# Top-two expert choice of 14 of 16 batches taken out of the routing and made in the last batch's attention

## What is computed

```
h = layernorm(x) * (1 + ca) + sa
x = x + ga * attention(h)                      # softmax attention, per batch
h = layernorm(x) * (1 + cb) + sb
logits = h @ Wr + br                           # 8192 tokens x 8 experts
top_vals, top_idx = top_k(logits, 2)
w = softmax(top_vals)                          # two weights per token
key = where(expert was chosen, w, -1e30)       # 8 x 8192 in effect
kv, ki = top_k(key, 1280)                      # each expert's tokens
y = (gelu(h[tok] @ W1 + b1) @ W2 + b2) * gate  # scattered back and added
x = x + gb * layernorm(y_sum + h) ...
```

## Time and profile before

| what | value |
| --- | --- |
| time, median of 3 runs | 1362.34 us (1360.73 to 1362.84) |
| time of the profiled execution | 1361.43 us |
| its span | 1359.7 us |
| busy: TensorE, VectorE, ScalarE, GpSimd | 86%, 73%, 56%, 71% of the span |
| granted TensorE clock, mean | 0.917 of full |

### The profile page before, as it was taken

The page is one execution under the profiler, slowest core; times in us unless marked ns, Lnnn a source line. Parts: engine busy times, 40 slices in busy tenths (PEclk is TensorE's granted clock), DMA queues, the critical chain, the costliest instruction groups (busy, mean ns, idle before and its releaser), DMA issues. The chain is left out here.

```text
span 1359.7 us, 23684 instructions
## 1 busy us (share of the span) xinstructions
PE 1163.7 (86%) x5975; PEld 786.6 (58%) x5976; DVE 989.6 (73%) x2189; ACT 757.9 (56%) x1494; POOL 958.7 (71%) x1096
## 2 busy tenths in 40 slices
PE   7899999999999999999999999999972175989400
PEld 6456566665656666665656666665542175989400
DVE  4888687777768777777767777776637894767596
ACT  4665666566566766666566765666422531444244
POOL 4686978888796878878697878879651135545268
PEclk9999999999999999999999999999985556999755
DMA  4000101011010101011010101010014203233374
GB/s 152 17 19 17 57 8 63 3 62 42 20 47 16 63 0 62 16 47 47 16 47 16 62 0 48 8 42 32 17 47 132 70 0 94 46 95 47 93 251 165
DMA packets 68478, 70.91 MB, mean 52 GB/s; under 512 B 12912, under 2 KB 64032, under 8 KB 68272
## 3 DMA queue, kind: packets, MB, share of 16 engines
q1 hardware_dynamic: 46800, 47.18, 10.9%
q10 hardware_dynamic: 16896, 16.78, 3.7%
q0 software_dynamic: 4704, 6.11, 3.0%
HBM read 40.35 MB, written 29.45 MB: 51 GB/s over the span
## 5 line engine op out<-in xcount | busy, mean ns | idle before, releaser
L627 ACT ACTIVATE PF<-PS 128x512 f32<-128x512 f32 x512 | 298.2, 595 | 256.6 <-PE PS L1002 248.4
L894 DVE TENSOR_REDUCE NMAX<-PS 128x1 f32<-128x512 f32 x512 | 342.7, 682 | 87.7 <-PE PS L1011 84.4
L490 POOL TENSOR_TENSOR SF<-SF,PF 128x512 f32<-128x512 f32 x252 | 321.9, 1298 | 14.9 <-ACT PF L627 14.7
L1083 PE MATMUL PS<-PF,V 128*64 128x512 f32 x1024 | 248.0, 605 | 0.0
L1001 PE MATMUL PS<-Q,K 128*128 128x512 f32 x512 | 222.1, 434 | 2.7 <-ACT PF L627 2.6
L1011 PE MATMUL PS<-K,Q 128*128 128x512 f32 x512 | 205.6, 403 | 10.4 <-DVE NMAX L894 10.3
L1002 PE MATMUL PS<-Q,K 128*128 128x512 f32 x512 | 201.3, 393 | 0.0
L646 ACT ACTIVATE Q<-PS 64x512 fp32r<-64x512 f32 x256 | 151.5, 592 | 47.5 <-PE PS L102 42.5
L568 POOL TENSOR_TENSOR XL<-XF,XH 128x512 fp32r<-128x512 f32 x63 | 82.6, 1311 | 128.1 <-ACT XH L701 128.1
L1001 PEld LDWEIGHTS PS<-Q,K 128*128 128x128 f32 x512 | 96.3, 188 | 120.2 <-issue 55.2
L487 POOL TENSOR_TENSOR SF<-PF 128x512 f32<-128x512 f32 x126 | 162.0, 1301 | 2.9 <-ACT PF L627 2.9
(11 more groups left out here) (329 smaller groups left out, 2501.1 us busy)
## 6 DMA issues: line engine op xcount, KB each, us to landing
X<-in_L_attn_x SPq DMA_DIRECT2D x16, 512.0 KB, 3.5
MODB<-mod_rows SPq DMA_DIRECT2D x16, 512.0 KB, 3.7
h_rows<-H ACTq DMA_DIRECT2D x16, 512.0 KB, 3.0
acc_rows<-H ACTq DMA_DIRECT2D x16, 512.0 KB, 4.1
out_x<-X SPq DMA_DIRECT2D x16, 512.0 KB, 2.9
A<-acc_rows SPq DMA_DIRECT2D x15, 512.0 KB, 8.7
W1F<-in_L_ffn_W SPq DMA_DIRECT2D x3, 1024.0 KB, 5.0
W2F<-in_L_ffn_W SPq DMA_DIRECT2D x3, 1024.0 KB, 7.3
```

The costliest lines, as they stand in the source:

```text
L490: s_sum.done(pool.tensor_tensor(total, total, tile, ALU.add))
L627: s_exp.done(act.activation(PF[:, u % 8, :], st_bank(u), ACT.Exp))
L894: s_mred.done(dve.tensor_reduce(NMAX[:, p % 2, r:r + 1], mx_bank(u), AX.X, ALU.max, negate=True))
L1083: last = pe.matmul(num_bank(p)[odd * R:(odd + 1) * R, :], V1[:, vp, c, :], PF[:, k % 8, :], start=(c == 0), stop=(c == TC - 1))
```

## The change

- `LOGITS` is now laid out as 4 chunks x 16 batches x 8 experts, so that a range of batches is a slice of it; L884 writes at that stride.
- The top-two chain is a class `TopTwo` of 20 steps, 0 to 19, over a range of batches. Its last step writes the keys over the logits; `KEY` is gone.
- `early` does batches 0 to 13 (448 elements wide, 56 narrow) in the attention: steps 0 to 12 in body 15, one a slot from slot 19, and steps 13 to 19 in body 16, slots 0 to 3, two a slot. Its tiles lie in tiles of the attention that are free by then. Each step stands at the start of its slot on VectorE, ahead of the slot's jobs and divisions, and waits for the step before. Its exponential is in ScalarE's body 15, slot 28.
- `late` does batches 14 and 15 in the routing, in 64 elements wide, 8 narrow.
- The keys are released by one semaphore increment after the last step. TensorE and SyncE read them from `LOGITS`.
- GpSimd waits at the start of the routing until the last batch's H2 has been read by its transfers (`s_h2out`).

```diff
+EARLY = NB - 2
+class TopTwo:
+    STEPS, EXP_FROM, EXP_TO = 20, 7, 12
+    def exponential(self, act):
+        act.wait_ge(self.s_dd, 1)
+        act.activation(self.ex, self.den, ACT.Exp).then_inc(self.s_exp, 1)
+    def step(self, dve, k, link):
+        L, eq, oh1, oh2, l2 = self.logits, self.eq, self.oh1, self.oh2, self.l2
+        if k == 0:
+            link(dve.tensor_reduce(self.m1, L, AX.X, ALU.max))
+        elif k == 1:
+            link(dve.tensor_tensor(eq, L, self.each(self.m1), ALU.is_equal))
+        elif k == 2:
+            link(dve.tensor_tensor(eq, eq, self.rank, ALU.mult))
+        elif k == 3:
+            link(dve.tensor_reduce(self.i1, eq, AX.X, ALU.max))
+        elif k == 4:
+            link(dve.tensor_tensor(oh1, self.rank, self.each(self.i1), ALU.is_equal))
+        elif k == 5:
+            link(dve.scalar_tensor_tensor(out=l2, in0=oh1, scalar=-3.0e38, in1=L, op0=ALU.mult, op1=ALU.add))
+        elif k == 6:
+            link(dve.tensor_reduce(self.m2, l2, AX.X, ALU.max))
+        elif k == 7:
+            link(dve.tensor_tensor(self.den, self.m2, self.m1, ALU.subtract))
+            dve.sem_inc(self.s_dd, 1)
+        elif k == 8:
+            link(dve.tensor_tensor(eq, l2, self.each(self.m2), ALU.is_equal))
+        elif k == 9:
+            link(dve.tensor_tensor(eq, eq, self.rank, ALU.mult))
+        elif k == 10:
+            link(dve.tensor_reduce(self.i2, eq, AX.X, ALU.max))
+        elif k == 11:
+            link(dve.tensor_tensor(oh2, self.rank, self.each(self.i2), ALU.is_equal))
+        elif k == 12:
+            dve.wait_ge(self.s_exp, 1)
+            link(dve.tensor_scalar(self.den, self.ex, 1.0, None, ALU.add))
+        elif k == 13:
+            link(dve.reciprocal(self.w1, self.den))
+        elif k == 14:
+            link(dve.tensor_tensor(self.w2, self.ex, self.w1, ALU.mult))
+        elif k == 15:
+            link(dve.tensor_tensor(eq, oh1, oh2, ALU.add))
+        elif k == 16:
+            link(dve.tensor_tensor(oh1, oh1, self.each(self.w1), ALU.mult))
+        elif k == 17:
+            link(dve.tensor_tensor(oh2, oh2, self.each(self.w2), ALU.mult))
+        elif k == 18:
+            link(dve.tensor_tensor(oh1, oh1, oh2, ALU.add))
+        elif k == 19:
+            link(dve.scalar_tensor_tensor(out=L, in0=eq, scalar=-1.0, in1=oh1, op0=ALU.add, op1=ALU.add))
...
+    TOP_AT, TOP_EXP = [(NB - 1, 19 + k) for k in range(13)] + [(NB, k // 2) for k in range(7)], (NB - 1, 28)
...
+                    if at == TOP_EXP:
+                        early.exponential(act)
...
+                    for k in [k for k in range(TopTwo.STEPS) if TOP_AT[k] == at]:
...
+                        early.step(dve, k, top)
                     normalise(b, n, 0)
...
     @block.gpsimd
     def _(pool):
+        m["s_h2out"].wait(pool, NB - 1, 1)
         pool.memset(ONES[:, :], 1.0).then_inc(s_pool, 1)
...
-        sp.wait_ge(s_key, TC)
+        sp.wait_ge(s_key, 1)
...
-            sp.dma_start(rows[q], KEY[:, q, :, :]).then_inc(s_tab, 16)
+            sp.dma_start(rows[q], LOGITS[:, q, :, :]).then_inc(s_tab, 16)
...
+        for k in range(TopTwo.STEPS):
+            late.step(dve, k, link)
+        dve.sem_inc(s_key, 1)
         dve.wait_ge(s_pool, POOL_CONSTS)
-        for q in range(TC):
-            dve.scalar_tensor_tensor(out=KEY[:, q, :, :], in0=EQ[:, q::TC, :], scalar=-1.0, in1=OH1[:, q::TC, :],
-                                     op0=ALU.add, op1=ALU.add).then_inc(s_key, 1)
```

More of the change, by code:

```diff
@@ L83, in wait, with __init__, each @@
         eng.wait_ge(self.sem, b * 8 + (16 - 8 * self.parity))
+class TopTwo:
+    STEPS, EXP_FROM, EXP_TO = 20, 7, 12
+    def __init__(self, m, batches, wide, small, s_dd, s_exp):
+        self.b, self.n = batches, batches.stop - batches.start
+        self.logits = m["LOGITS"][:, :, batches, :]
+        self.eq, self.oh1, self.oh2, self.l2 = (x.rearrange("p (q b e) -> p q b e", q=TC, e=E) for x in wide)
+        self.m1, self.m2, self.i1, self.i2, self.ex, self.w1, self.w2, self.den = (x.rearrange("p (q b) -> p q b", q=TC) for x in small)
+        self.rank = m["RANK8"][:, :].unsqueeze(1).unsqueeze(1).broadcast_to([P, TC, self.n, E])
+        self.s_dd, self.s_exp = s_dd, s_exp
+    def each(self, x):
+        return x.unsqueeze(3).broadcast_to([P, TC, self.n, E])
+    def exponential(self, act):
[45 more added lines that the diff above has]
+            link(dve.scalar_tensor_tensor(out=L, in0=eq, scalar=-1.0, in1=oh1, op0=ALU.add, op1=ALU.add))
@@ L120, in build_program @@
         m["IDENT"] = sb("IDENT", [P, P])
[L121 removed]
+        m["LOGITS"] = sb("LOGITS", [P, TC, NB, E])
         m["SAME"], m["LOWER"] = sb("SAME", [P, P]), sb("LOWER", [P, P])
@@ L231, in attention @@
     EPSC, HALF, ONE5, NEG1 = (m[x] for x in ("EPSC", "HALF", "ONE5", "NEG1"))
+    n4, n1 = TC * EARLY * E, TC * EARLY
+    flat = [x[:, :, :].rearrange("p k n -> p (k n)") for x in (NF, XN1)]
+    s_top = sem("s_top")
+    early = TopTwo(m, slice(0, EARLY), [x[:, j * n4:(j + 1) * n4] for x in flat for j in range(2)],
+                   [LTF[:, j * n1:(j + 1) * n1] for j in range(8)], sem("s_topd"), sem("s_tope"))
+    TOP_AT, TOP_EXP = [(NB - 1, 19 + k) for k in range(13)] + [(NB, k // 2) for k in range(7)], (NB - 1, 28)
     streams = []
@@ L761, in finish @@
                         dve.tensor_tensor(H2[:, c, :], H2[:, c, :], MODB[:, 2, :], ALU.add).then_inc(s_hadd2, 1)
-            chain, mask, pad = Chain(dve, s_dset), Chain(dve, s_mask), Chain(dve, s_keypad)
+            chain, mask, pad, top = Chain(dve, s_dset), Chain(dve, s_mask), Chain(dve, s_keypad), Chain(dve, s_top)
             pad(dve.memset(K2[R:P, :, :].bitcast(F32), 0.0))
@@ L1122, in route @@
     FAR = 4.0 * NT
-    EQ, OH1, OH2, L2 = (sb(x, [P, NCH, E]) for x in ("EQ", "OH1", "OH2", "L2"))
-    KEY = sb("KEY", [P, TC, NS, E])
-    M1, M2, I1, I2, EX, W1, W2, DEN = (sb(x, [P, NCH]) for x in ("M1", "M2", "I1", "I2", "EX", "W1", "W2", "DENr"))
+    EQ, n1 = sb("EQ", [P, NCH, E]), TC * (NB - EARLY)
+    wide, small = [sb(x, [P, n1 * E])[:, :] for x in ("EQt", "OH1", "OH2", "L2")], [
+        sb(x, [P, n1])[:, :] for x in ("M1", "M2", "I1", "I2", "EX", "W1", "W2", "DENr")]
     HI, LO, LOW, SGN, EQT, RANK, SEL, SCAN, DST, ZT = (
@@ L1161, in route @@
     m["s_tab"] = s_tab
+    late = TopTwo(m, slice(EARLY, NB), wide, small, sem("s_rtopd"), s_exp)
     kt_ps = PS[:, 0, :]
@@ L1205, in _ @@
         act.activation(iot_ps, IOT[:, :], ACT.Copy).then_inc(s_iot, 1)
-        act.wait_ge(s_dd, 1)
-        act.activation(EX[:, :], DEN[:, :], ACT.Exp).then_inc(s_exp, 1)
+        late.exponential(act)
         act.wait_ge(s_split, 1)
@@ L1259, in _ @@
     def _(pe):
-        pe.wait_ge(s_key, TC)
+        pe.wait_ge(s_key, 1)
         for q in range(TC):
-            last = pe.transpose(kt_ps[:, q * P:(q + 1) * P], KEY[:, q, :, :].rearrange("p c e -> p (c e)"), IDENT[:, :])
+            last = pe.transpose(kt_ps[:, q * P:(q + 1) * P], LOGITS[:, q, :, :].rearrange("p c e -> p (c e)"), IDENT[:, :])
         last.then_inc(s_kt, 1)
```

30 lines of the change are left out of this document (6 added, 24 removed).

## The result

| | before | after |
|---|---|---|
| time, median of 7 runs each | 1362.34 us (1360.44 to 1363.08) | 1357.64 us (1356.31 to 1360.08) |
| ratio after/before, 95% interval | | 0.997 (0.9959 to 0.9981) |
| span of the profiled execution | 1359.7 us | 1355.4 us |
| last pair of score maxima starts at | 978.10 | 978.56 |
| from there to the routing's first step | 47.78 us | 52.14 us |

The forecast was 1358.0 us, with 3.6 us more in the attention and 7.9 us less in the routing.

The account below looks back on a forecast made before the run. The serial top-two chain, 13.28 us with only VectorE working, was taken to bound the edited place. Routing 7.9 us less, attention 3.6 more: 4.3 less, 1357.1 from the profiled run, 1358.0 forecast; own range 1356.3 to 1359.7.

Parts of the forecast that it names:

- The routing, 7.9 us less: From the first routing step to the key transposes: 5.35 us in place of 13.28, by narrower steps.
- GpSimd's new wait, 0 us: At the routing's start, GpSimd waits for batch 15's outgoing rows before its constants: no cost, with 3.8 us of cover.
- The early block, 3.6 us: In the attention, early steps and GpSimd's products exclude each other: the last pair's transpose and the attention's end 3.6 us later.
- Step 2: In the early block, waits for GpSimd's product until 984.7; XF of pair 1 ends 2.4 us late, costing 0.
- Step 1: In the early block, falls with step 0 in VectorE's 3.34 us gap before pair 1's transpose: free.
- Steps 12 to 19: Early block's end, after XF of pair 2: 6.2 us to 1006.0, with steps 14, 15 and 16 waiting for GpSimd.
- Nothing behind absorbs it: After the last pair's transpose: the whole 3.6 us delay reaches the attention's end; TensorE gap of some 2 us before the projection.
- Kept after 1040: Behind the routing the chain is serial (digits, list, experts, last norm), so what is taken out is kept.
- Whole-instruction exclusion: Rival: VectorE and GpSimd exclude each other for whole instructions; attention 5.7 us late, 2.2 less in all, 1360.1; chance 0.1.
- no exclusion: Rival: early steps fall into gaps without exclusion that matters; 0.5 us late, 7.4 less in all, 1354.9; chance 0.12.
- The gain is given back: Rival: a wait behind the gain or an unluckier clock phase among the experts gives back 3 us, 1361; chance 0.13.
- The clock falls in the tail: Rival: TensorE stalls bring the clock's fall before 997; work to 1007.2 takes 10.3 us more, 1366.1; chance 0.05.

Follow-up runs that it names:

- e1: Changed kernel without its early block, all 16 batches chosen in the routing with the new layout and wait: 1363.13 us, 1.0003 of before.
- e2: Changed kernel with the early block's last step writing to a spare buffer and the routing choosing for all 16 batches: 1368.12 us, 1.0038 of before.
- e3: e2 with early steps that have two SBUF inputs replaced by reductions of as many elements: 1362.08 us, 0.9991 of before.
- e7: e6 with the ranks in PSUM too, I1 and I2 back in SBUF, step 12's addition writing to PSUM: 1355.62 us, 0.9948 of before.
- e6: Changed kernel with the edits of e4 and e5 together: 1355.48 us, 0.9951 of before; its second run 1354.98 us, 0.9948.
- e5: Changed kernel with five of the early block's eight narrow operands in PSUM: 1358.33 us, 0.9966 of before.
- e4: Changed kernel with early steps moved to other slots, none inside a division: 1356.60 us, 0.9958 of before.
- e8: Changed kernel with eight batches chosen early and eight in the routing: 1359.87 us, 0.9981 of before.

## Why the prediction was right

Its steps, one by one:

The sum came out at the size that was measured, and the mechanism held; that 4.3 is met to a tenth by the two spans is luck. The two terms that it was made of measure 8.12 and 4.36, which leaves 3.76; the other 0.54 are the 1.00 gained behind the routing less the 0.46 of a later start, and no term stood for either.

- **The routing, 7.9 us less.** Measured 8.12 (13.28 - 5.16). The sum of 5.35 was 0.19 too high: narrow steps took 0.17 (L126) and the reciprocal 0.20, as forecast, and nothing was held by GpSimd, for which 0.15 stood in the sum. The exponential stayed hidden.
- **GpSimd's new wait, 0 us.** In its timeline of after the constants come at 1030.65 to 1032.10. They start 0.05 us before the routing's first step, as they do in the kernel before (0.04), and nothing waits for them before the transposes at 1035.86. e1 shows the same in the time. To the letter a sign of being wrong has come true, "a GpSimd constant later than 1031"; but 1031 is where the keys would end without the attention's delay (1025.88 + 5.35), and in after they end at 1035.76, 3.7 us behind the last constant.
- **The early block, 3.6 us.** Measured 4.01 to the last pair (e2 over e1 gives 4.01 and, over the whole stretch, 4.03). e3 confirms the cause. Most of the missed 0.4 is no fault of the walk through the queues: at the logits of batch 14 that gave 3.55 late (1006.0 for 1002.45), and 3.66 was measured. The rest is mostly the short gap of 0.28 us before the last pair's transpose, which no term stood for. The parts were less exact than the sum. The three largest:
  - *Step 2 was to wait* for GpSimd, 1.7 us in all (the 2.4 less step 3's 0.66). It began first, took 0.70, and stretched GpSimd's L564 to 1.66. XF of pair 1 was 1.2 late, not 2.4. Nobody waited for it, so nothing came of the error.
  - *Step 1 was called free.* It was not: through L550 it made TensorE 0.4 us late (idle 1.23, for 0.85 in e3 and e7 and in the kernel before). With it the h2 transposes of chunk 1 and chunk 3 were 1.3 and 1.9 late, not 0.7 and 1.4, and XF of pair 2 2.8 late, not 2.5. This term is missing in the sum, and it is luck that so little of it is seen at the end: steps 12 to 19 gave 0.2 back. The prediction also counts thirteen steps with two inputs in SBUF; there are fourteen, step 1 among them. Its fault was to look only for who waits for VectorE, and not for which of GpSimd's short instructions, with who waits for them, stands beside the step.
  - *Steps 12 to 19, 6.2 us.* Measured 6.06 (from L138 at 1000.51 to L970 at 1006.57). The waits fell one step later than forecast: step 14 (L142) was not held (0.22 for 1.32), and step 15 (L144) took 1.57.
- **Nothing behind absorbs it.** Right: TensorE waits 1.98 us for XL before the last projection; "some 2 us" was forecast.
- **Kept after 1040.** Right within 1 us: the span is 4.30 shorter, with 1.00 more than the two terms and the later start give. The granted clock differs among the experts (0.59 before and 0.99 after from 1150 to 1155, 0.95 and 0.83 from 1140 to 1145; these stretches hold work that is 3 to 4 us apart); how much of the 1.00 is due to that, no run separates.

The rivals:

- *Whole-instruction exclusion* (5.7 us) and *no exclusion* (0.5 us): 4.0 lies between them, as forecast. The first is the Trainium skill's rule on SBUF — State Buffer, Who interferes with whom: the second to issue is blocked for the whole instruction. This trace agrees on who excludes whom and not on how long, and the walk rightly went by the trace. L564, begun 0.18 us after L116, was longer by 0.39, where the rest of L116 was 0.52.
- *The gain is given back*: not seen.
- *The clock falls in the tail*: not where it was feared, and its cost is 0.3 us, not 10. The grant stays full until 1010, and the work of the tail runs at it up to the very end of the projection. There it does fall, ahead of the last three matmuls, and earlier in the work than before, though TensorE had been busy just as little. So the sign "a grant below full before the projection" holds for those three matmuls alone. The 3.00 us from the first YT addition (L869 of before, L955 of after), the same work in both; first before, then after (the columns are us, busy us by engine, granted clock, transfers' share, GB/s):

```profile
1007.26:1010.26 3.00, 0.90 (x7) 0.49 (x5) 2.81 (x10) 0.00 (x0) 0.00 (x0) 1.00 0.00 0
```

```profile
1011.74:1014.74 3.00, 0.90 (x7) 0.49 (x5) 2.81 (x10) 0.00 (x0) 0.00 (x0) 0.80 0.00 0
```

**Two short gaps.** Of the 4.36 us that the stretch is longer than before, 0.35 us stand behind the last pair's transpose, nearly all of it a gap before the YT addition of the last chunk (L955), in VectorE's timeline of after:

```profile
1015.82 0.42 DVE L955 TENSOR_TENSOR YT<-PS,MODB 128x256 f32<-128x256 f32 x1 [0.23 <-issue]
```

No wait is named, but this addition reads what TensorE's last three matmuls of the projection write, and these were slower. TensorE's timeline of after, then of e6 and of its second run:

```profile
1014.72 0.58 PE L170 MATMUL PS<-GH,XH 128*128 128x256 f32 x1 [1.88 <-DVE YT L955]
```

```profile
1012.60 0.39 PE L170 MATMUL PS<-GH,XH 128*128 128x256 f32 x1 [1.87 <-DVE YT L955]
```

```profile
1012.12 0.58 PE L170 MATMUL PS<-GH,XH 128*128 128x256 f32 x1 [1.88 <-DVE YT L955]
```

The same matmul takes 0.58 at a granted clock of 0.50 (after, and the second run of e6) and 0.39 at 1.00 (e6). The first profile of e6 has no gap (1013.38, above), its second has

```profile
1013.22 0.42 DVE L955 TENSOR_TENSOR YT<-PS,MODB 128x256 f32<-128x256 f32 x1 [0.24 <-issue]
```

All twelve profiles agree: where this matmul takes 0.56 to 0.58 (both of after, e1, e2, e5, e7, the second of e6) the gap of 0.21 to 0.24 us is there, and where it takes 0.38 or 0.39 (before, e3, e4, e8, the first of e6) it isn't. So it is no property of the change: the clock falls before or behind these matmuls, in two executions of one kernel too.

**What stays open.** The like gap of 0.28 us before the last pair's L815 stands in both profiles of after, in e2, e3, e5, e7 and e8, and not in before, e1, e4 and both of e6. The clock was full there, and both kernels that were profiled twice repeat it; what makes it, no run shows. It is 0.3 us of what e4 and e6 gain over the changed kernel in the table.

## What to carry to other kernels

Idle time of VectorE is free only for instructions that don't need what GpSimd is reading through: beside a busy GpSimd, count a step with two SBUF inputs at the length of GpSimd's product and lengthen that product too, and ask who waits for each of GpSimd's instructions, the short ones first. Put one operand of such a step in PSUM, or use a reduction, and it costs its own time again; place what is left ahead of a dependent chain and not between its parts. Work taken out of a serial chain and into an overlapped one is worth the difference of two terms, and each can be measured by itself by doing the work in both places.

## What the runs showed of the hardware that I had not expected

- **An addition of a constant is held too.** L138 adds 1.0 to 56 elements, one input in SBUF, output in SBUF. Alone it takes 0.18 (after). Beside a GpSimd product it took 0.60 (e4) and 1.06 (e6): there it ended 0.04 us after GpSimd's XL product (993.71 to 994.99). With its output in PSUM it took 0.22 beside a busy GpSimd (e7). The Trainium skill (SBUF — State Buffer, Who interferes with whom) says that such an instruction can enter a mode that takes both ports and then contends; these rows agree.
- **One input in PSUM is enough to escape**: 0.61, 0.62 and 0.22 where the same steps took 1.16 (e4's L120), 1.51 and 0.79. GpSimd's products beside them keep their 1.27.
- **A gap that is listed with no wait can be TensorE's clock.** The 0.21 to 0.24 us before L955 came and went between executions of the same kernel (0 and 0.24 for e6) with the clock that was granted to the three matmuls in front of it. In a study of changes worth a few us such gaps are a part of the error.
